# Linear attention's weight preparation moved to GpSimd and to earlier layers of a four-layer decoder

## The chip, the cores and the metric

The kernel runs on one core of one Trainium2 chip, as one launch. The metric is the device time of one execution in microseconds. Three runs of the kernel before took 2272.78, 2275.60 and 2278.18 us; the median is 2275.6.

## The reference

Four decoder layers run over x, 8 sequences of 128 tokens by 256 features in fp32. Each layer adds three sublayers to x, each of the layer-normalised x. The change touches three that follow each other:

- **L1_ffn** (the expert stage): a shared gated feed-forward and seven routed ones, top 3 by a softmax router; the gates weigh the experts' outputs.
- **L2_attn** (ALiBi attention): 16 heads of 16, causal, with a slope per head.
- **L2_xattn** (called linear attention below, after its quantised linear layers): `ln_out` is quantised four times, `y = clip(ln_out / in_scale, -448, 448)` rounded to bf16 and then to the grid of float8 e4m3, for q, qx, k and v. Then q, k, v, qx are linear in those, k and v of the context `kx, vx` are linear in `cond`; q, k, qx and kx are layer-normalised per head of 128; 16 heads attend to 8 k/v groups, once to the sequence and once to the context; both results are quantised again and multiplied by `wproj`.

```
q  = ln(fp8_linear(ln_out, wq, wq_scale, q_in_scale))      # 16 heads x 128
k  = ln(fp8_linear(ln_out, wk, wk_scale, k_in_scale))      #  8 heads x 128
xq = round_fp8(clip(x / in_scale)); fp8_linear = (xq * in_scale) @ w.T * w_scale
out = quantise(concat(core, xout), proj_smooth) @ wproj.T * (proj_in_scale * proj_w_scale)
```

The kernel folds `in_scale * w_scale` into the weights, and takes each head's mean out of the weights (centring) so that the layer norm of q, k, qx and kx needs only a sum of squares.

## The kernel before

One program per engine is written out by hand; engines meet at semaphores only. Each engine runs its list in order, so the order of the lines is the order of the work. SyncE (SP) issues all DMAs from one queue. Names: L1f is the expert stage, L2a ALiBi attention, L2x linear attention.

**Expert stage (L1f).** Four passes `b` over two sequences each. PE does gate/up and down products for eight experts; ACT the SiLU; DVE the products, the router's small tensors (7 columns: L2703 to L2748, among them L2734) and the weighted sums. GpSimd has no part in it. In its time GpSimd runs `L2x_split` (L1183 to L1194) for the eight pieces `q` of the output weight `wproj`: cast to bf16 (`hi`), subtract, cast (`mid`), subtract, cast (`lo`), so that three bf16 matmuls stand for one of fp32. The pieces come through two buffers `p_raw`; SP loads piece q when `lo` of q - 2 is done.

**ALiBi attention (L2a).** A software pipeline of nine iterations; the sequence is the index. On GpSimd iteration i is norm(i + 2) (L1204), then two subtractions of the row maximum (L1208), one for each half of the heads. ACT: copies of transposed tiles, two exp (L1743), the copy of the next normalised sequence (L1725). DVE: bias (L2831), maximum (L2837), reciprocal (L2841), scale, residual (L2849). PE: scores, transposes, products, projection (L4049). At its end PE, DVE and POOL wait for all of it.

**Linear attention (L2x).** First an opening: DVE takes sequence 0's statistics and normalises it (`L2x_stats`, `L2x_u`), PE transposes, ACT scales (`L2x_unT`), DVE and GpSimd quantise it four times in turn (`L2x_quantise`, four DVE instructions; `L2x_quantise_sum`, two on GpSimd, L1226 and L1228). ACT scales the weights of step j (`L2x_scale_weights`, L1788 and L1791, one head at a time with a sum), DVE subtracts the means (`L2x_centre_weights`, L2898 to L2904). Steps 0 and 1 are in the opening, steps 2 to 7 in iterations 0 to 5 of the loop.

Then 64 iterations (n = i // 8 is the sequence, i % 8 the group of heads, own keys for the first four and context keys for the others). In an iteration: project q, k, v (L4096, L4100, L4108), squares on ACT and their sum on DVE (L2925), rstd, norm, transposes, scores, exp (L1844), `L2x_prob` on GpSimd (L1232), product with v, `L2x_smooth` (DVE, L2947 to L2955, rounding the output), `L2x_cat` (GpSimd, L1238, L1240), and the projection of iteration i - 3 with the three bf16 weights (L4157). In iterations with i % 8 from 3 to 6 DVE and GpSimd quantise the next sequence.

SP (L964 to L992) loads the weights of L2x into the place of the expert stage's weights, so it waits for that stage's last matmuls and last vector work; the ten loads were issued between 747.5 and 756.5 us.

Of the kernel before, what the change touches and what calls it, by code (L numbers as in the profile page):

```python
# [108 lines left out]
def build_program(nc, dram, out_d):  # L109
# [89 lines left out]
    with stack:  # L199
# [259 lines left out]
        w_q2 = view(sbuf, 18376, [2, 2048])  # L459
        w_qx2 = view(sbuf, 22472, [2, 2048])  # L460
        w_k2 = view(sbuf, 14274, [2, 1024])
        w_v2 = view(sbuf, 16322, [2, 1024])
        w_kv2 = view(sbuf, 26568, [2, 2048])
        p_raw = [view(sbuf, 11520 + 1024 * p, [4, 256]) for p in range(2)]
        w_p3 = [view(sbuf, 30664 + 4096 * p, [32, 256], BF16) for p in range(3)]
# [6 lines left out]
        wsum = view(sbuf, 42984, [2, 12])  # L472
        wmean = view(sbuf, 43008, [2, 12])
# [8 lines left out]
        L2a_P = [view(sbuf, 46152 + 1024 * a, [8, 128]) for a in range(2)]  # L482
# [14 lines left out]
        L2a_u = view(sbuf, 44040, [256])  # L497
# [32 lines left out]
        wps = view(sbuf, 52838, [1])  # L530
# [13 lines left out]
        L2x_uT = view(psum, 3840, [2, 128])  # L544
        L2x_qT = view(psum, 1024, [4, 128])
# [286 lines left out]
        rest_done = stack.enter_context(nc.semaphore('rest_done'))  # L832
        L2x_w_loaded = stack.enter_context(nc.semaphore('L2x_w_loaded'))
# [23 lines left out]
        def _(sp):  # L857
# [99 lines left out]
            sp.dma_start(w_dn1[:, :, :, :], w_dn1_d).then_inc(L1f_w_loaded, 16)  # L957

# [22 lines left out]
            sp.wait_ge(L1f_w_loaded, 112)  # L981
            sp.dma_start(w_k2[:, :, :], w_k2_d).then_inc(L2x_w_loaded, 16)
            sp.wait_ge(L1f_matmul_done, 138)
            sp.dma_start(w_v2[:, :, :], w_v2_d).then_inc(L2x_w_loaded, 16)
            sp.wait_ge(L1f_w_loaded, 112)
            sp.wait_ge(L1f_vector_done, 221)
            sp.dma_start(w_kv2[:, :, :], w_kv2_d).then_inc(L2x_w_loaded, 16)
            sp.dma_start(insc[:, :, :], insc_d).then_inc(L2x_w_loaded, 16)
# [12 lines left out]
            sp.wait_ge(L0f_w_loaded, 64)  # L1001
            sp.dma_start(w_q2f[:, :], w_q2f_d).then_inc(L2f_w_loaded, 16)
# [52 lines left out]
        def _(pool):  # L1055
# [127 lines left out]
            def L2x_split(q):  # L1183
                part = slice(4 * q, 4 * q + 4)
                pool.wait_ge((L2x_p0_loaded, L2x_p1_loaded)[q % 2], 16 * (q // 2) + 16)
                pool.tensor_copy(w_p3[0][:, part, :], p_raw[q % 2][:, :, :]).then_inc(hi_done, 1)
                pool.wait_ge(hi_done, L2x_start['hi'] + q + 1)
                pool.tensor_tensor(p_raw[q % 2][:, :, :], p_raw[q % 2][:, :, :], w_p3[0][:, part, :], ALU.subtract).then_inc(rest_done, 1)
                pool.wait_ge(rest_done, 2 * q + 1)
                pool.tensor_copy(w_p3[1][:, part, :], p_raw[q % 2][:, :, :]).then_inc(mid_done, 1)  # L1190
                pool.wait_ge(mid_done, L2x_start['mid'] + q + 1)
                pool.tensor_tensor(p_raw[q % 2][:, :, :], p_raw[q % 2][:, :, :], w_p3[1][:, part, :], ALU.subtract).then_inc(rest_done, 1)
                pool.wait_ge(rest_done, 2 * q + 2)
                pool.tensor_copy(w_p3[2][:, part, :], p_raw[q % 2][:, :, :]).then_inc(lo_done, 1)  # L1194

            pool.wait_ge(resid_done, L1x_start['resid'] + 8)
            for q in range(8):
                L2x_split(q)
# [18 lines left out]

            pool.wait_ge(L0f_w_loaded, 64)
            pool.wait_ge(proj_done, L2a_start['proj'] + 8)
            pool.memset(keys[:, :, :], 0.0).then_inc(L2f_keys_zeroed, 1)  # L1220
# [23 lines left out]
            for i in range(67):  # L1244
# [4 lines left out]
                if i < 56 and i % 8 in (3, 4, 5, 6):  # L1249
                    L2x_quantise_sum(4 * (i // 8 + 1) + i % 8 - 3)  # L1250

# [84 lines left out]
        def _(act):  # L1336
# [379 lines left out]

            def L2a_rstd(a, b, c):
# [54 lines left out]
            act.wait_ge(L2x_w_loaded, 160)  # L1772

            def L2x_scale_weights(j):
                act.wait_ge(const_done, L2x_start['const'] + 1)
                if j >= 2:
                    act.wait_ge(centred_done, L2x_start['centred'] + j - 1)
                g, part = j % 4, j // 4
                wq, vq = (w_q2, 0) if part == 0 else (w_qx2, 1)
                wk = w_k2 if part == 0 else w_kv2  # L1780
                if part == 0:
                    for c in range(2):
                        w = w_v2[:, c, 256 * g:256 * g + 256]
                        act.activation(w, w, ACT.Copy, scale=wfs[:, 3, c:c + 1])
                for c in range(2):
                    for h in range(4):
                        w = wq[:, c, 512 * g + 128 * h:512 * g + 128 * h + 128]
# [70 lines left out]
            for i in range(66):  # L1858
# [12 lines left out]
                if i < 6:  # L1871
                    L2x_scale_weights(i + 2)
# [2911 lines left out]
```

## Time and profile before

| what | value |
|---|---|
| median of three runs | 2275.6 us |
| the profiled execution's own time | 2279.39 us |
| its span, first to last instruction | 2277.6 us |
| mean granted TensorE clock, share of full | 0.927 |
| busy: PE, DVE, ACT, POOL | 1897.8, 1494.5, 1111.4, 1027.5 us |
| expert stage's four passes | 575.5 to 754.3 us |
| ALiBi attention | 754.3 to 852.5 us |
| linear attention: opening, then 64 iterations | 852.5 to 872.4, then to about 1450 us |
| splitting of the output weight on GpSimd | 575.4 to 636.7 us |

Busy time is the time in which an engine carries out instructions. The granted clock is the share of its full speed that TensorE was given. The chain of work that ended last, over the whole span, is PE 45%, DVE 22%, issue 12%, ACT 11%, POOL 9%.

### The profile page before, as it was taken

Reading aid. Unit: us, or ns where it says so; the run is one execution under the profiler, and the core shown is the slowest. Engines: PE = TensorE matmul, PEld = TensorE weight load, DVE = VectorE, ACT = ScalarE, POOL = GpSimd, SP = SyncE. Lnnn points to the kernel's source line nnn. Section 1 sums busy time; section 2 is a strip of 40 time slices with the busy share of each in tenths; the row PEclk is TensorE's granted clock in tenths of the full one; section 3 lists DMA queues with packets and bytes.
Section 4 is the critical chain, followed back from the end, with each engine's and each line's share of the span. In section 5 each row is a group of like instructions: output and inputs, shape, how many; then the busy total and the mean of one; then the engine's idle time right before and its main releaser. Section 6 shows DMA issues by size and latency. Waiting matters only on the chain.

```text
span 2277.6 us, 32744 instructions
## 1 busy us (share of the span) xinstructions
PE 1897.8 (83%) x11446; PEld 1395.2 (61%) x11446; DVE 1494.5 (66%) x2588; ACT 1111.4 (49%) x2532; POOL 1027.5 (45%) x734
## 2 busy tenths in 40 slices
PE   7677788787999875699999999768888789977999
PEld 6111166544899663577777777657777665544888
DVE  5698933475654573566666666569999958756443
ACT  4444422253232346666565665556766536633443
POOL 2699921121910331344454444479999920012231
PEclk9688888698999996899999999989999989998999
DMA  4111001201100301000000000100000020000000
GB/s 153 42 33 33 0 1 72 111 0 56 56 0 0 149 5 55 1 1 1 1 1 1 1 1 22 34 1 1 1 1 1 26 76 1 1 0 1 6 8 8
DMA packets 22164, 54.82 MB, mean 24 GB/s; under 512 B 8463, under 2 KB 13752, under 8 KB 19592
## 3 DMA queue, kind: packets, MB, share of 16 engines
q1 hardware_dynamic: 22024, 53.01, 7.0%
q8 instruction: 81, 1.33, 0.2%
q14 instruction: 59, 0.48, 0.1%
HBM read 44.61 MB, written 1.05 MB: 20 GB/s over the span
## 4 chain that ended last, share of the span: by engine, by line
PE 45%; DVE 22%; issue 12%; ACT 11%; POOL 9%; SPq 1%; DMA 0%; DVEq 0%; POOLq 0%; ACTq 0%
POOL sbuf L1270 4%; DVE sbuf L2255 3%; PE psum L4096 3%; DVE sbuf L2925 3%; PE psum L4157 2%; POOL sbuf L1278 2%; PE psum L3475 2%; ACT sbuf L1844 2%; PE psum L4144 2%; DVE psum L3060 1%; PE psum L4583 1%; PE psum L4604 1%; PE psum L4590 1%; DVE sbuf L2917 1%; PE psum L4100 1%
## 5 line engine op out<-in xcount | busy, mean ns | idle before, releaser
L1270 POOL TENSOR_TENSOR sbuf<-sbuf 128x1035 f32<-128x1035 f32 x128 | 248.4, 1971 | 0.9 <-ACT sbuf L1912 0.9
L4230 PE MATMUL psum<-sbuf 128*128 128x128 f32 (+1 forms) x1024 | 143.3, 290 | 58.7 <-ACT sbuf L1921 43.0
L1921 ACT ACTIVATE sbuf<-sbuf 128x1001 f32<-128x1001 f32 (+1 forms) x128 | 141.6, 1139 | 100.8 <-DVE sbuf L3068 65.0
L4230 PEld LDWEIGHTS psum<-sbuf 128*128 128x128 f32 (+1 forms) x1024 | 125.6, 152 | 79.8 <-ACT sbuf L1921 58.1
L1232 POOL TENSOR_TENSOR sbuf<-sbuf 128x512 f32<-128x512 f32 x64 | 69.6, 1087 | 217.2 <-DVE sbuf L2942 217.2
L1111 POOL TENSOR_TENSOR sbuf<-sbuf 128x1024 f32<-128x1024 f32 x64 | 149.9, 2354 | 16.1 <-DVE sbuf L2255 15.2
L2255 DVE TENSOR_TENSOR_SCAN sbuf<-psum,sbuf 128x1024 f32<-128x1024 f32 x64 | 144.5, 2278 | 14.0 <-POOL sbuf L1111 7.7
L3423 PE MATMUL psum<-sbuf 96*128 96x512 bf16 x256 | 83.9, 439 | 74.3 <-DVE sbuf L2255 33.1
L4096 PE MATMUL psum<-sbuf 128*128 128x512 f32 x256 | 124.3, 609 | 17.4 <-DVE sbuf L2904 17.4
L3060 DVE SCALAR_TENSOR_TENSOR psum<-sbuf,psum 128x1024 f32<-128x1024 f32 (+1 forms) x96 | 122.3, 1274 | 14.2 <-PE psum L4220 7.0
L1391 ACT ACTIVATE psum<-psum,sbuf 128x1016 f32<-128x1016 f32 x64 | 68.9, 1081 | 125.5 <-PE psum L3423 125.5
L1844 ACT ACTIVATE sbuf<-psum,sbuf 128x128 f32<-128x128 f32 x256 | 90.7, 366 | 77.1 <-DVE sbuf L2936 77.1
L3068 DVE TENSOR_TENSOR sbuf<-psum,sbuf 128x1024 f32<-128x1024 f32 (+1 forms) x96 | 116.4, 1213 | 3.3
L4144 PE MATMUL psum<-sbuf 128*128 128x256 f32 x256 | 74.3, 414 | 52.0 <-ACT sbuf L1851 52.0
L3423 PEld LDWEIGHTS psum<-sbuf 96*128 96x128 bf16 x256 | 19.0, 104 | 152.5 <-DVE sbuf L2255 62.5
L1238 POOL TENSOR_TENSOR sbuf<-sbuf 128x512 f32<-128x512 bf16 x64 | 74.3, 1161 | 68.2 <-DVE sbuf L2955 66.5
L4157 PE MATMUL psum<-sbuf 128*128 128x256 bf16 x768 | 98.2, 280 | 5.0 <-POOL sbuf L1240 5.0
L4157 PEld LDWEIGHTS psum<-sbuf 128*128 128x128 bf16 x768 | 76.8, 100 | 24.1 <-POOL sbuf L1240 6.1
L1325 POOL TENSOR_TENSOR sbuf<-sbuf 128x1024 f32<-128x1024 f32 x16 | 30.3, 1915 | 129.6 <-DVE sbuf L3315 129.6
L2925 DVE TENSOR_REDUCE sbuf<-sbuf 128x6 f32<-128x768 f32 x64 | 60.8, 950 | 38.4 <-ACT sbuf L1814 38.4
L4144 PEld LDWEIGHTS psum<-sbuf 128*128 128x128 f32 x256 | 44.5, 194 | 67.5 <-ACT sbuf L1851 63.9
L1240 POOL TENSOR_TENSOR sbuf<-sbuf 128x512 bf16<-128x512 f32 x64 | 81.3, 1271 | 5.0
(899 smaller groups left out, 5153.6 us busy)
## 6 DMA issues: line engine op xcount, KB each, us to landing
sbuf<-sbuf SPq DMA_DIRECT2D x42, 128.0 KB, 2.4
sbuf<-w_p_d SPq DMA_DIRECT2D x8, 512.0 KB, 3.6
sbuf<-w_qkv_d SPq DMA_DIRECT2D x3, 768.0 KB, 4.3
sbuf<-w_e_d SPq DMA_DIRECT2D x1, 2048.0 KB, 7.7
sbuf<-w_gu_d SPq DMA_DIRECT2D x1, 2048.0 KB, 9.4
sbuf<-w_gu_d SPq DMA_DIRECT2D x2, 1024.0 KB, 7.9
sbuf<-w_dn_d SPq DMA_DIRECT2D x1, 2048.0 KB, 16.4
sbuf<-w_q_d SPq DMA_DIRECT2D x1, 2048.0 KB, 8.3
```

The lines of the kernel that those rows point to most:

```text
L1111: pool.tensor_tensor(L0a_hc[i % 4][:, :], L0a_hs[i % 2][:, :], L0a_Cr[g % 4][:, :], ALU.mult).then_inc(hc_done, 1)
L1270: pool.tensor_tensor(P_r[g % 7][:, :, :], rows.unsqueeze(2).to_broadcast([128, 23, 45]), cols.unsqueeze(1).to_broadcast([128, 23, 45]), AL ...
L1844: last = act.activation(prob[:, h, :], L2x_s[:, h, :], ACT.Exp, bias=smax[:, h:h + 1], accum_out=esum[:, h:h + 1])
L1921: act.activation(Q_r[g % 6][:, 0:w], Q_r[g % 6][:, 0:w], ACT.Silu, scale=q8_p[n % 2][:, h:h + 1]).then_inc(silu_done, 1)
L2255: dve.tensor_tensor_scan(L0a_hs[i % 2][:, :], L0a_dAf[i % 2][:, :], L0a_us[i % 3][:, :], 0.0, ALU.mult, ALU.add).then_inc(scan_done, 1)
L2925: dve.tensor_reduce(ssum[:, :], sq[:, :, :], AX.X, ALU.add).then_inc(ss_done, 1)
L3060: dve.scalar_tensor_tensor(M[:, 0:w], Pf_r[g % 7][:, o:o + w], t8_p[n % 2][:, h, 7:8], zps[:, 0:w], ALU.is_ge, ALU.mult).then_inc(mask_don ...
L3068: dve.tensor_tensor(Q_r[g % 6][:, 0:w], Mps[:, 0:w], Pf_r[g % 7][:, o:o + w], ALU.mult).then_inc(prod_done, 1)
L4096: last = pe.matmul(L2x_q[:, :, :], xs[:, vq, c, :], wq[:, c, 512 * g:512 * g + 512], start=c == 0, stop=c == 1)
L4144: last = pe.matmul(L2x_o[:, 2 * h:2 * h + 2, :], v2_r[i % 3][:, h, :], pT2[:, 2 * h:2 * h + 2, :], start=True, stop=True)
L4157: last = pe.matmul(L2x_out[:, :], cat16[:, h, :], w_p3[p][:, 4 * (i % 8) + h, :], start=i % 8 == 0 and h == 0 and p == 0, stop=i % 8 == 7 ...
L4230: last = pe.matmul(Gps[0:m, c, :], Q_r[g % 6][:, 128 * c:128 * c + m], ident[:, :], start=h == 0 and c % 4 == 0, stop=h == 7, skip_group_c ...
```

## The change

- **Scaling and centring** of w_v, w_k, w_q, w_qx and w_kv leave ACT and DVE; GpSimd does all of it after the ALiBi table, in the time of the expert stage. A scale is one product over 8 or 16 heads of 128; a mean is a tree of seven additions in place of ACT's running sum.
- **The split** of the output weight is shared: casts `hi` and `mid` on ACT, subtractions `rest` and `lo` on GpSimd (`lo` writes bf16 at once, its own cast is gone). Pieces 0 to 3 go into the iterations of ALiBi attention, 4 to 7 into iterations 0 to 7 of linear attention, one of `rest` and `lo` an iteration.
- **Sequence 0**: statistics in DVE's iteration 3 of ALiBi attention, u(0) and copies 0 and 1 in iteration 7, copies 2 and 3 in iteration 8; the transpose goes to another PSUM tile. PE's wait for the whole of ALiBi attention goes.
- **Buffers**: the L2x weights move behind the expert stage's, so they are loaded once L1_xattn's residuals are done; the split weight takes the place of the expert stage's weights. Two buffers of ALiBi attention move.
- **SP**: insc, wsc, w_k and w_v are issued with the expert stage's own weights; pieces 2 to 7 of the output weight come behind the L2x weights, and the loads of the next layer (L997 on) behind them. `keys` is zeroed in iteration 8 of linear attention.

```diff
-        w_q2 = view(sbuf, 18376, [2, 2048])
+        w_q2 = view(sbuf, 30664, [2, 2048])
-        w_p3 = [view(sbuf, 30664 + 4096 * p, [32, 256], BF16) for p in range(3)]
+        w_p3 = [view(sbuf, 18376 + 4096 * p, [32, 256], BF16) for p in range(3)]
 SP
+            sp.dma_start(w_k2[:, :, :], w_k2_d).then_inc(L2x_c_loaded, 16)
+            sp.dma_start(w_v2[:, :, :], w_v2_d).then_inc(L2x_c_loaded, 16)
...
-            sp.wait_ge(L1f_matmul_done, 130)
+            sp.wait_ge(resid_done, L1x_start['resid'] + 8)
             sp.dma_start(w_q2[:, :, :], w_q2_d).then_inc(L2x_w_loaded, 16)
...
+            for q in range(2, 8):
+                sp.wait_ge(lo_done, L2x_start['lo'] + q - 1)
+                sp.dma_start(p_raw[q % 2][:, :, :], w_p2_d[:, 4 * q:4 * q + 4, :]).then_inc((L2x_p0_loaded, L2x_p1_loaded)[q % 2], 16)
 GpSimd
+            def L2x_scale(j, w, factor):
+                pool.tensor_tensor(w, w, factor.unsqueeze(2).to_broadcast([128, w.shape[1], 128]), ALU.mult).then_inc(scaled_done, 1)
+            def L2x_centre(j, w, heads):
+                pool.tensor_tensor(wtree[:, 0:heads, 0:64], w[:, :, 0:64], w[:, :, 64:128], ALU.add).then_inc(sums_done, 1)
+                for s in range(6):
+                    half = 32 >> s
+                    pool.wait_ge(sums_done, L2x_start['sums'] + 8 * j + s + 1)
+                    pool.tensor_tensor(wtree[:, 0:heads, 0:half], wtree[:, 0:heads, 0:half], wtree[:, 0:heads, half:2 * half], ALU.add).then_inc(sums_done, 1)
...
+                pool.tensor_scalar(wmean[:, 0:heads], wtree[:, 0:heads, 0], -1.0 / 128.0, None, ALU.mult).then_inc(sums_done, 1)
...
+                pool.tensor_tensor(w, w, wmean[:, 0:heads].unsqueeze(2).to_broadcast([128, heads, 128]), ALU.add).then_inc(centred_done, 1)
...
+            def L2x_rest(q):
+                part = slice(4 * q, 4 * q + 4)
                 pool.wait_ge(hi_done, L2x_start['hi'] + q + 1)
                 pool.tensor_tensor(p_raw[q % 2][:, :, :], p_raw[q % 2][:, :, :], w_p3[0][:, part, :], ALU.subtract).then_inc(rest_done, 1)
+            def L2x_lo(q):
...
+                pool.tensor_tensor(w_p3[2][:, part, :], p_raw[q % 2][:, :, :], w_p3[1][:, part, :], ALU.subtract).then_inc(lo_done, 1)
 GpSimd, ALiBi attention, end of iteration i
                 L2a_sub(i, 0)
                 L2a_sub(i, 1)
+                if i % 2 == 0:
+                    L2x_rest(i // 2)
+                else:
+                    L2x_lo(i // 2)
 ACT, ALiBi attention, end of iteration i
+                if i % 2 == 0:
+                    if i == 0:
+                        act.wait_ge(L1f_matmul_done, 138)
+                    L2x_hi(i // 2)
+                else:
+                    L2x_mid(i // 2)
+                if i == 5:
+                    L2x_factor(0)
+                if i == 7:
+                    act.wait_ge(L2x_w_loaded, 96)
+                    L2x_unT(0)
 ACT, linear attention
-                if i < 6:
-                    L2x_scale_weights(i + 2)
+                if i % 2 == 1 and i < 8:
+                    L2x_mid(4 + i // 2)
+                    if i < 7:
+                        L2x_hi(5 + i // 2)
 GpSimd, linear attention, end of iteration i
+                if i < 8:
+                    if i % 2 == 0:
+                        L2x_rest(4 + i // 2)
+                    else:
+                        L2x_lo(4 + i // 2)
 DVE, ALiBi attention
+                if i == 7:
+                    L2x_u(0)
                 if i > 0:
                     L2a_scale(i - 1)
                     L2a_resid(i - 1)
+                if i == 7:
+                    L2x_quantise(0)
+                    L2x_quantise(1)
...
+                if i == 8:
+                    L2x_quantise(2)
+                    L2x_quantise(3)
 PE
-            pe.wait_ge(resid_done, L2a_start['resid'] + 8)
...
-                if n == 0:
-                    pe.wait_ge(centred_done, L2x_start['centred'] + i + 1)
+                if i == 0:
+                    pe.wait_ge(centred_done, L2x_start['centred'] + 8)
...
-                if i == 0:
-                    pe.wait_ge(lo_done, L2x_start['lo'] + 8)
+                if i < 8:
+                    pe.wait_ge(lo_done, L2x_start['lo'] + i + 1)
```

## Rows read from the trace of the kernel before

**Rows 1.** The page's busy time, share of span and instructions by engine.
```profile
PE 1897.8 (83%) x11446; PEld 1395.2 (61%) x11446; DVE 1494.5 (66%) x2588; ACT 1111.4 (49%) x2532; POOL 1027.5 (45%) x734
```

**Rows 2.** Windows by stage: us, busy by engine, granted clock, DMA share.
```profile
575.50:622.70 47.20, 44.40 (x334) 41.89 (x333) 30.35 (x62) 11.63 (x30) 45.38 (x32) 1.00 0.22 58
622.70:667.10 44.40, 43.20 (x327) 41.07 (x326) 24.29 (x62) 11.34 (x29) 13.48 (x9) 1.00 0.03 10
667.10:710.90 43.80, 43.80 (x335) 41.86 (x334) 19.73 (x63) 11.76 (x29) 0.00 (x0) 1.00 0.00 0
...
754.30:852.50 98.20, 78.83 (x976) 63.32 (x976) 66.86 (x86) 43.60 (x69) 40.41 (x25) 0.94 0.16 66
852.50:872.40 19.90, 0.66 (x2) 0.29 (x2) 9.26 (x31) 12.06 (x56) 6.57 (x9) 0.50 0.53 167
872.40:975.50 103.10, 73.73 (x311) 53.55 (x312) 52.30 (x113) 63.94 (x269) 24.43 (x25) 0.81 0.00 1
975.50:1044.70 69.20, 63.19 (x373) 49.37 (x372) 46.64 (x93) 41.65 (x133) 34.21 (x33) 1.00 0.00 1
```

**Rows 3.** Waits, 852 to 976 us: total us, times, longest.
```profile
DVE sbuf L2898 <- ACT sbuf L1791: 25.8, 6, 5.2
...
PE psum L4096 <- DVE sbuf L2904: 17.4, 1, 17.4
```

**Rows 4.** Groups of instructions, 852 to 976 us: busy us, mean ns.
```profile
L1788 ACT ACTIVATE sbuf<-sbuf 128x128 f32<-128x128 f32 x64 | 24.8, 397 | 0.0
```

**Rows 5.** Timeline of PE: start us, us, line; the first projection.
```profile
872.42 3.78 PE L4096 MATMUL psum<-sbuf 128*128 128x512 f32 x4 [17.45 <-DVE sbuf L2904]
```

**Rows 6.** Timeline of DVE and GpSimd in the opening.
```profile
852.05 0.42 DVE L2849 TENSOR_TENSOR sbuf<-psum,sbuf 128x256 f32<-128x256 f32 x1 [1.70 <-PE psum L4049]
...
867.56 0.72 POOL L1228 TENSOR_TENSOR sbuf<-sbuf 128x256 f32<-128x256 f32 x1
```

**Rows 7.** Timeline of ACT and GpSimd in ALiBi attention.
```profile
775.52 1.05 ACT L1743 ACTIVATE sbuf<-sbuf 128x1024 f32<-128x1024 f32 x1
...
784.27 1.05 ACT L1743 ACTIVATE sbuf<-sbuf 128x1024 f32<-128x1024 f32 x1
...
788.78 1.90 POOL L1208 TENSOR_TENSOR sbuf<-sbuf 128x1024 f32<-128x1024 f32 x1 [3.84 <-DVE sbuf L2837]
...
793.51 1.22 POOL L1204 TENSOR_SCALAR sbuf<-sbuf 128x256 f32<-128x256 f32 x1
...
793.88 1.05 ACT L1743 ACTIVATE sbuf<-sbuf 128x1024 f32<-128x1024 f32 x1
...
794.82 0.38 ACT L1725 ACTIVATE sbuf<-psum 128x256 f32<-128x256 f32 x1
```

**Rows 8.** Timeline of GpSimd and DVE in the expert stage.
```profile
575.43 1.03 POOL L1186 CAST sbuf<-sbuf 128x1024 bf16<-128x1024 f32 x1
...
576.55 2.13 POOL L1188 TENSOR_TENSOR sbuf<-sbuf 128x1024 f32<-128x1024 f32 x1
...
584.17 2.14 POOL L1188 TENSOR_TENSOR sbuf<-sbuf 128x1024 f32<-128x1024 f32 x1
584.28 2.06 DVE L2734 TENSOR_TENSOR sbuf<-sbuf 128x7 f32<-128x7 f32 x1
...
676.40 0.17 DVE L2734 TENSOR_TENSOR sbuf<-sbuf 128x7 f32<-128x7 f32 x1
```

**Rows 9.** Timeline of GpSimd and DVE in linear attention.
```profile
1069.28 1.04 POOL L1232 TENSOR_TENSOR sbuf<-sbuf 128x512 f32<-128x512 f32 x1 [3.38 <-DVE sbuf L2942]
...
1080.41 0.81 POOL L1228 TENSOR_TENSOR sbuf<-sbuf 128x256 f32<-128x256 f32 x1
...
1080.67 0.70 DVE L2953 TENSOR_SCALAR sbuf<-sbuf 128x512 uint16<-128x512 uint16 x1
...
1081.75 0.94 DVE L2925 TENSOR_REDUCE sbuf<-sbuf 128x6 f32<-128x768 f32 x1
```

**Rows 10.** DMA issues, 440 to 760 us: KB each, us to landing.
```profile
sbuf<-w_kv_d SPq DMA_DIRECT2D x1, 2048.0 KB, 16.2
```

More of the change, by code:

```diff
@@ L481, in build_program @@
         L2a_table = view(sbuf, 9472, [2, 8, 128])
-        L2a_P = [view(sbuf, 46152 + 1024 * a, [8, 128]) for a in range(2)]
+        L2a_P = [view(sbuf, 3328 + 1024 * a, [8, 128]) for a in range(2)]
         L2a_PT = [view(sbuf, 48200 + 1024 * a, [8, 128]) for a in range(2)]
@@ new lines, in _ @@
+            for c in range(2):
+                pool.wait_ge(scaled_done, L2x_start['scaled'] + 3 + c)
+                L2x_centre(c, L2x_heads(w_k2[:, c, :]), 8)
+            pool.wait_ge(L2x_w_loaded, 96)
+            for c in range(2):
+                L2x_scale(4 + c, L2x_heads(w_q2[:, c, :]), wfs[:, 0, c:c + 1])
+            for c in range(2):
+                pool.wait_ge(scaled_done, L2x_start['scaled'] + 5 + c)
+                L2x_centre(2 + c, L2x_heads(w_q2[:, c, :]), 16)
+            for c in range(2):
+                L2x_scale(6 + c, L2x_heads(w_qx2[:, c, :]), wfs[:, 1, c:c + 1])
@@ L1184, in L2x_split @@
+            for c in range(2):
+                pool.wait_ge(scaled_done, L2x_start['scaled'] + 7 + c)
+                L2x_centre(4 + c, L2x_heads(w_qx2[:, c, :]), 16)
+            for c in range(2):
+                L2x_centre(6 + c, L2x_heads(w_kv2[:, c, 0:1024]), 8)
+            def L2x_rest(q):
                 part = slice(4 * q, 4 * q + 4)
-                pool.wait_ge((L2x_p0_loaded, L2x_p1_loaded)[q % 2], 16 * (q // 2) + 16)
-                pool.tensor_copy(w_p3[0][:, part, :], p_raw[q % 2][:, :, :]).then_inc(hi_done, 1)
@@ L1193, in L2x_split @@
[L1193 to L1198, printed above, removed]
+                pool.tensor_tensor(w_p3[2][:, part, :], p_raw[q % 2][:, :, :], w_p3[1][:, part, :], ALU.subtract).then_inc(lo_done, 1)
             def L2a_norm(n):
@@ L1771, in _ @@
                     L2a_unTc(i + 2)
[L1772 to L1787, printed above, removed]
-                        act.activation(w, w, ACT.Copy, scale=wfs[:, vq, c:c + 1], accum_out=wsum[:, j % 2, 4 * c + h:4 * c + h + 1])
-                    for h in range(2):
-                        w = wk[:, c, 256 * g + 128 * h:256 * g + 128 * h + 128]
-                        last = act.activation(w, w, ACT.Copy, scale=wfs[:, 2, c:c + 1] if part == 0 else 1.0, accum_out=wsum[:, j % 2, 8 + 2 * c + h:9 + 2 * c + h])
-                last.then_inc(scaled_done, 1)
@@ L3989, in _, with L2x_uTr @@
                 last.then_inc(L1f_matmul_done, 1)
+            def L2x_uTr(n):
+                pe.wait_ge(u_done, L2x_start['u'] + n + 1)
+                out = L2x_uT_first if n == 0 else L2x_uT
+                for c in range(2):
+                    last = pe.transpose(out[:, c, :], u0[:, 128 * c:128 * c + 128], ident[:, :])
+                last.then_inc(uT_done, 1)
             def L2a_uTr(n):
@@ L4073, in _ @@
                     L2a_project(i - 1)
-            pe.wait_ge(resid_done, L2a_start['resid'] + 8)
-            def L2x_uTr(n):
-                pe.wait_ge(u_done, L2x_start['u'] + n + 1)
-                for c in range(2):
-                    last = pe.transpose(L2x_uT[:, c, :], u0[:, 128 * c:128 * c + 128], ident[:, :])
-                last.then_inc(uT_done, 1)
+                if i == 7:
+                    L2x_uTr(0)
             def L2x_project(i):
```

180 lines of the change are left out of this document (82 added, 98 removed).

## The prediction

> **What bounds the kernel now.** I read the stages first. The page gives PE as the busiest engine, 83% of a span of 2277.6 us [rows 1], but an average over twelve layers prices nothing. The table of windows [rows 2] cuts out the stretch that the change touches: the four passes of the expert stage (575.5 to 754.3 us), ALiBi attention (754.3 to 852.5), the opening of linear attention (852.5 to 872.4) and its 64 iterations. Two rows stand out. In the opening PE is busy 0.66 of 19.9 us. The first eight iterations take 103.1 us where the next eight take 69.2, though both do the same attention work and both quantise the sequence that follows; PE's granted clock is 0.81 in the first and full in the second. So 19.9 + 33.9 = 53.8 us are spent on what the change moves: scaling and centring the weights, and quantising sequence 0.
>
> The waits of that stretch say who makes the time [rows 3]. PE waits 17.4 us for the first centred group (L2904), and DVE's centring (L2898) waits 25.8 us for ACT's scaling, which is 96 short instructions with an accumulator read behind each; 64 of them (L1788) alone are 24.8 us plus their reads [rows 4]. ACT is the bound there; after the weights are done its load is gone.
>
> **The change, part by part.** All sums are against the profiled execution (span 2277.6 us, 2279.4 us with what lies around it); the median of the runs is 2275.6, 3.8 us lower, and a difference worked out on the trace is taken off the median.
>
> *1. Weights out of the first eight iterations: -32.7 us.* From the first projection, at 872.42 [rows 5], to the ninth, at 975.5, are 103.1 us [rows 2]. Eight iterations without weights take 69.2 [rows 2]; I add 1.2 for the first, which starts on a slow clock (3.78 us for its first four matmuls, [rows 5]), and get 70.4. The difference is 32.7. Bounds of the 70.4: 68 (a pipeline that fills is shorter) and 76 (the clock stays at 1.2 GHz for two iterations).
>
> *2. Sequence 0 quantised inside ALiBi attention: -13.6 us.* Before, the last residual ends at 852.47 and the third quantised copy, the one that the first projection waits for, then as now, at 868.28 [rows 6]; centring brings the start to 872.42. After, u(0), the transpose and copies 0 and 1 stand in iterations 7 and 8. They aren't free: the fourth `lo` on GpSimd has two SBUF inputs, and the first copy's DVE multiply has too, so by the kind of wait in [rows 8] it starts when `lo` ends, near 847.4. That copy is 1.3 us, its GpSimd sum 1.5, and copy 1's second half (0.9) waits for it, so DVE reaches the last normalisation at 851.3 where it stood at 848.1, +3.2 us. Residual 7 ends at 855.7, copy 2 takes 1.4 and its sum 1.5 more, and the projection starts at 858.8 instead of 872.4. Bounds 11 and 17 (the latter if DVE comes through copy 1 before attention's last product is ready).
>
> *3. Split of the output weight inside ALiBi attention: +6.2 us.* Nothing here is a bound engine: GpSimd is busy 40 and ACT 44 of 98 us [rows 2]. But GpSimd runs in order. In iteration i it now does norm(i+2), two subtractions, then `rest` or `lo`, which wait for a cast on ACT that stands behind exp(i,1) and the copy L1725. Queued behind that wait is norm(i+3), then the subtraction that iteration i+1 needs. From [rows 7]: exp(i,1) at 793.88, L1725 ends at 795.20, cast 1.05 (an ACT pass over 1024 elements, as exp), GpSimd from 796.3, 2.14 for `rest` (as L1188, [rows 8]), norm 1.22, so the subtraction starts at 799.6, where today it comes 9.8 us behind the one at 788.78, at 798.6. From the subtraction to the next exp(i,1) are 5.1 us, as from 788.78 to 793.88: the loop through ACT and GpSimd is 10.8 us with `rest` and some 11.0 with `lo`, against 9.8 us. It binds where a norm is in it, in the steps to iterations 1 to 5: 2.1 for the first (8.75 before, 784.27 less 775.52), 1.1 for each of four, 6.5, of which PE's idle time ahead of the projection L4049 gives back some 0.5 (an estimate); u(0) adds 0.35 in iteration 7, the reciprocals and the statistics fall into idle time of DVE (0.68 us an iteration). Bounds 0.5 (GpSimd's norm slips through; no gain, since nothing is taken out of these iterations) and 9.
>
> *4. Scaling and centring on GpSimd in the expert stage: +4 us.* Work: 1 + 8 + 8 x 9 = 81 instructions over 36,768 elements a partition. By L1208 (1024 elements, 1.90 us, [rows 7]) and L1232 (512, 1.04, [rows 9]) an element costs 1.68 ns and an instruction 0.18, and 0.09 lies between two that depend on each other (576.46 to 576.55, [rows 8]): 84 us, from 575.5 to 660. It replaces 61 us of splitting and ends 94 us before ALiBi attention needs anything, so GpSimd's own time is free. What isn't free is DVE. In pass 0, under the split, one DVE product of 7 elements (L2734) takes 2.06 us, exactly until GpSimd's instruction ends; in pass 2, with GpSimd idle, it takes 0.17 [rows 8]. Over a pass that is 30.35 us of DVE against 19.73, and the pass is 47.2 us against 43.8; pass 1, covered for 14 us, is 44.4 [rows 2]. So the split costs 3.4 + 0.6 us now and 10.6 us of blocking turns into 3.4 of time. After, the k weights' short sums lie beside pass 0's routing (cheaper, about -2), but two shared products at its end and pass 1's whole routing meet instructions of 2048 elements, 3.6 us each. I take -1 for pass 0 and +5 for pass 1. Bounds -2 and +9.
>
> The row shows an exclusive wait, and the Trainium skill (SBUF — State Buffer, Who interferes with whom) says the same: GpSimd and a DVE instruction with two SBUF inputs, or in a two-port mode, hold the pair for a whole instruction. By that rule a wait grows with the length of GpSimd's instruction, which speaks against this change; were it of one size whatever the instruction, this term would be near 0 and the sum -29. The trace agrees with the rule: 2.06 us beside an instruction of 2.14.
>
> *5. The second half of the split inside linear attention: +11 us.* In iterations 0 to 7 GpSimd runs `rest` or `lo` (2.1 to 2.4 us) right behind the quantising sum. DVE then has the smoothing's three conversions (L2951, L2953, L2955), all SBUF to SBUF. Now L2953 takes 0.70 us because it waits for L1228, and the sum of squares L2925 follows at 1081.75 without a pause [rows 9]. With `rest` behind L1228, L2955 waits till 1083.4 and L2925 starts 2.1 us later, and it is on the path (chain: L2925, L1851, then PE). That is 4 x 2.2 for iterations 3 to 6, 0.8 each for 2 and 7, where DVE has a pause, and 0.7 for ACT's two casts in iteration 1: 11. Bounds: 3 (DVE's three conversions pass first; 0.4 each in eight iterations) and 17 (both delays in every iteration).
>
> *6. Transfers: 0.* The weights' 6 MB leave at 571 instead of 747.5; the last landed 16.2 us after issue [rows 10], before GpSimd gets to w_q at 594. If it were late, GpSimd has 94 us to spare. Queue SP is now held by `lo` until iteration 5 of linear attention before the next layer's weights; they have 500 us.
>
> Sum: -32.7 - 13.6 + 6.2 + 4 + 11 = -25.1, from the median 2275.6: **2250.5 us**.
>
> **Rivals.**
> *A. The cover holds* (terms 3 and 5 mostly hidden): GpSimd is idle 58 us of ALiBi attention [rows 2], and if casts and subtractions slip into the gaps, terms 3 to 5 are 1, 1 and 4, and the time is 2235. Against it: GpSimd's order, and the gaps are after the norm, not ahead of it.
> *B. Contention costs more*: 9 + 8 + 17 with -12 and -30 of gain, the clock low for a while: 2268. For it: PE's clock was 0.81 when its work was broken up [rows 2].
> *C. Slower.* In the expert stage each of some ten shared DVE instructions a pass waits for a GpSimd instruction of 3.6 us, and none of it is hidden, over two passes: 20 x 2.6 = 52 us of wait less 4 paid today, +48 in place of +4, and the time is 2294. It decides from +29 on. Against it: only a third of pass 0's blocking reached the pass, and 2048-element instructions are under half of GpSimd's time.
> *D. It doesn't do what it says*: something else holds the first projection (GpSimd still centring, a late transfer), and only the ACT load goes: within 4.5 us of 2275.6. GpSimd's 94 us of reserve speak against it.
>
> **How the numbers follow.** Forecast 0.52 (2242 to 2259), A 0.20, B 0.22, C 0.03, D 0.03. The range 2234 to 2264 holds A's centre and the near half of B. 0.2% is 4.5 us, about what a measurement of this kernel tells from no change: faster 0.94, same 0.03, slower 0.03.
>
> **What would show it.** Right: the first L4096 projection near 869 us of the span and the ninth near 950; no ACT scaling in linear attention; ALiBi attention's iterations at 10.8 to 11.0 us for the first five and 9.8 after; pass 1 of the experts at 48 to 50 us with long DVE waits at its tiny products; iterations 3 to 6 of linear attention near 11.2 us. Wrong: iterations there of 9.05 (term 5 is nothing), ALiBi iterations of 9.8 (term 3 is nothing), or a projection that starts before 860 or after 880.

## The result and the profile after

The changed kernel takes 2331.7 us (median of 4 runs, 2327.85 to 2338.36), the kernel before 2275.8 (median of 4, 2272.78 to 2278.18): a ratio of 1.0251, 95% interval 1.0226 to 1.0275. It is 56 us slower where 25 us faster was predicted, far outside the range of 2234 to 2264. The profiled execution took 2338.36 us, its span is 2336.6; before, 2279.4 and 2277.6.

The busy line of the page answers to [rows 1] and shows nothing of it. PE has the same work, ACT and DVE have less, and GpSimd is busy 57 us more.

```profile
PE 1897.1 (81%) x11446; PEld 1397.0 (60%) x11446; DVE 1481.4 (63%) x2547; ACT 1088.7 (47%) x2348; POOL 1084.5 (46%) x791
```

The windows by stage of the kernel after, with the columns of [rows 2], show it at once. The first four are the passes of the expert stage, the fifth has no counterpart in [rows 2], then come ALiBi attention with the opening, and the first and second eight iterations of linear attention:

```profile
576.40:619.20 42.80, 42.80 (x326) 40.86 (x325) 19.53 (x62) 11.21 (x29) 0.17 (x1) 1.00 0.38 149
619.20:663.00 43.80, 43.80 (x335) 41.87 (x334) 19.73 (x63) 11.75 (x29) 0.00 (x0) 1.00 0.00 0
663.00:706.70 43.70, 43.70 (x334) 41.77 (x334) 19.66 (x63) 11.75 (x29) 0.00 (x0) 1.00 0.00 0
706.70:751.90 45.20, 42.20 (x319) 39.92 (x317) 21.40 (x73) 13.53 (x32) 0.02 (x1) 1.00 0.00 0
751.90:838.30 86.40, 0.00 (x0) 0.00 (x0) 2.23 (x12) 0.00 (x0) 81.27 (x81) 0.51 0.00 0
838.30:945.50 107.20, 78.53 (x978) 63.49 (x978) 69.17 (x86) 51.70 (x80) 61.22 (x38) 0.93 0.07 21
945.50:1027.10 81.60, 64.04 (x310) 46.76 (x311) 51.18 (x83) 43.83 (x128) 42.78 (x35) 0.90 0.10 33
1027.10:1096.30 69.20, 63.19 (x372) 49.36 (x371) 47.38 (x91) 41.65 (x133) 35.56 (x33) 1.00 0.09 26
```

For 86.40 us PE executes nothing and GpSimd is the only engine with work worth naming. In the expert stage, where that work was to be, GpSimd has one product of 0.20 us and then 175 us of nothing. Its timeline says why; the bracket is the idle time ahead of an instruction and what ended it:

```profile
566.71 9.69 POOL L1176 TENSOR_SCALAR sbuf<-sbuf 128x128 f32<-128x128 f32 x16
576.37 0.20 POOL L1197 TENSOR_TENSOR sbuf<-sbuf 128x8 f32<-128x8 f32 x1
751.88 7.45 POOL L1180 TENSOR_TENSOR sbuf<-sbuf 128x1024 f32<-128x1024 f32 x4 [175.32 <-DVE sbuf L2920]
...
836.39 1.90 POOL L1191 TENSOR_TENSOR sbuf<-sbuf 128x1024 f32<-128x1024 f32 x1
838.27 1.24 POOL L1235 TENSOR_SCALAR sbuf<-sbuf 128x256 f32<-128x256 f32 x1
```

L1197 is the product wfs (input scale times weight scale, one factor for each weight), L1180 the first scaling, L1191 the last centring, L1235 the first normalising of ALiBi attention. Between wfs and the first scaling stands L1198, `pool.wait_ge(const_done, L2x_start['const'] + 1)`: GpSimd waits for its own product. But `const_done` counts constants of all layers. `L2x_start['const']` is 9, so the wait wants ten. wfs made the ninth; the tenth comes from L2920, the last of VectorE's clears for ALiBi attention, which VectorE reaches when the last expert pass is over. Before, wfs was VectorE's and stood behind that clear, so the tenth increment was always its own. The early increment also works the other way, which no time here shows: VectorE (L2922) and PE (L4062) wait for the ninth count, which was the clear's, and wfs now gives it 175 us before the clear runs. The waits of 575 to 840 us put the rest in one line each (total, times, longest):

```profile
POOL sbuf L1180 <- DVE sbuf L2920: 175.3, 1, 175.3
PEld psum L4026 <- POOL sbuf L1235: 91.1, 1, 91.1
PE psum L4026 <- POOL sbuf L1235: 90.7, 1, 90.7
```

The work itself, 751.88 to 838.27, is 86.4 us; the prediction had 84. Nothing stands beside it, because the next thing that every engine needs is the normalising queued behind it.

**Where the time went**, stage by stage (us, from starts in the traces: first pass, first normalising, first and ninth projection of linear attention, first transposition and last residual of the feed-forward layer behind it). The last five columns are experiments, told below.

| stretch | before | after | own count | no weights | norm first | both | best |
|---|---|---|---|---|---|---|---|
| expert passes, to the first normalising | 181.3 | 262.7 | 181.2 | 176.3 | 181.3 | 181.2 | 176.5 |
| to the first projection | 116.4 | 107.3 | 108.5 | 110.7 | 102.8 | 102.8 | 104.0 |
| first eight iterations | 103.1 | 81.6 | 77.4 | 77.1 | 80.0 | 71.3 | 71.3 |
| to the next layer | 499.4 | 499.4 | 500.6 | 500.9 | 501.0 | 501.8 | 501.0 |
| feed-forward layer | 378.7 | 386.2 | 383.9 | 383.1 | 383.2 | 381.0 | 383.5 |
| from there to the end | 424.0 | 423.9 | 424.0 | 424.2 | 424.0 | 423.9 | 425.7 |

After against before: +0.9 ahead of the passes, +81.4, -9.2, -21.5, 0, +7.5, -0.1, together the +59.0 of the two spans. The gains that were forecast are there (-30.7); 81.4 us of exposed GpSimd work lie over them.

### The profile page after: what moved, and what is told of

Its sections match the earlier page's. It is cut to its first block, busy times and chain, and to the rows that moved or that the text cites. A ratio compares the mean times of both kernels' runs of the same rounds, so it can differ in the third digit from the quotient of the medians.

```text
span 2336.6 us, 32570 instructions
## 1 busy us (share of the span) xinstructions
PE 1897.1 (81%) x11446; PEld 1397.0 (60%) x11446; DVE 1481.4 (63%) x2547; ACT 1088.7 (47%) x2348; POOL 1084.5 (46%) x791
## 4 chain that ended last, share of the span: by engine, by line
PE 43%; DVE 21%; POOL 13%; issue 12%; ACT 9%; SPq 1%; DMA 0%; DVEq 0%; POOLq 0%; ACTq 0%
POOL sbuf L1308 4%; DVE sbuf L2288 3%; DVE sbuf L2962 3%; PE psum L4119 3%; DVE psum L3082 2%; PE psum L4180 2%; PE psum L3497 2%; ACT sbuf L1879 2%; PE psum L4167 2%; PE psum L4605 1%; DVE sbuf L3090 1%; DVE sbuf L2870 1%; POOL sbuf L1316 1%; PE psum L4626 1%; PE psum L4612 1%
## 5 line engine op out<-in xcount | busy, mean ns | idle before, releaser
L4252 PEld LDWEIGHTS psum<-sbuf 128*128 128x128 f32 (+1 forms) x1024 | 130.5, 157 | 78.4 <-ACT sbuf L1954 59.4
L3090 DVE TENSOR_TENSOR sbuf<-psum,sbuf 128x1024 f32<-128x1024 f32 (+1 forms) x96 | 116.4, 1213 | 3.3
L1180 POOL TENSOR_TENSOR sbuf<-sbuf 128x1024 f32<-128x1024 f32 (+1 forms) x8 | 21.8, 2747 | 175.3 <-DVE sbuf L2920 175.3
L3476 PE MATMUL psum<-sbuf 128*32 128x512 f32 x256 | 81.4, 769 | 3.5 <-POOL sbuf L1107 3.5
```

What stands on the lines that cost most here:

```text
L3090: dve.tensor_tensor(Q_r[g % 6][:, 0:w], Mps[:, 0:w], Pf_r[g % 7][:, o:o + w], ALU.mult).then_inc(prod_done, 1)
L4252: last = pe.matmul(Gps[0:m, c, :], Q_r[g % 6][:, 128 * c:128 * c + m], ident[:, :], start=h == 0 and c % 4 == 0, stop=h == 7, skip_group_c ...
```

## The experiments

The theory (W): the wait on the shared count is the whole of the loss; with a count of its own the work runs beside the experts, and the forecast's sum holds. The rivals: GpSimd's work disturbs the other engines wherever it stands (C, the one of the prediction), or the early count does harm in itself.

**e1_own_count** gives wfs a count of its own: it counts on top of the four loads that it waits for, and the shared counter gets its tenth increment from a constant that VectorE computes in ALiBi attention:

```diff
-            pool.tensor_tensor(wfs[:, :, :], ..., ALU.mult).then_inc(const_done, 1)
-            pool.wait_ge(const_done, L2x_start['const'] + 1)
+            pool.tensor_tensor(wfs[:, :, :], ..., ALU.mult).then_inc(L2x_c_loaded, 1)
+            pool.wait_ge(L2x_c_loaded, 65)
...
-                    dve.tensor_tensor(wps[:, :], wsc[:, 4:5], wsc[:, 5:6], ALU.mult)
+                    dve.tensor_tensor(wps[:, :], wsc[:, 4:5], wsc[:, 5:6], ALU.mult).then_inc(const_done, 1)
```

> Only the count that GpSimd waits on is changed: its product of the scales counts on the semaphore of its own loads (65th count) instead of the const_done shared with ALiBi attention, whose count for this stage is given by VectorE's product wps in ALiBi attention. Theory W (the loss is GpSimd's wait on the shared count, 576 to 752, with the whole of the weights' work after it): GpSimd works on the weights from 576 to about 660-665 beside the expert passes, the first normalising starts near 756-760 instead of 838, the first projection near 867, and the time falls by about 78-82 us from 2332, to 2250-2254. Theory C (GpSimd's work on the weights disturbs VectorE and ScalarE wherever it stands): the expert passes stretch by 20 us or more, the time is 2275-2295.

Measured: 2249.2 us (before 2274.4 beside it; ratio 0.9882, 0.9865 to 0.9900). The same GpSimd lines as above, now 92.94 us of rest behind the work instead of 175 ahead of it:

```profile
573.62 0.20 POOL L1197 TENSOR_TENSOR sbuf<-sbuf 128x8 f32<-128x8 f32 x1
573.89 7.45 POOL L1180 TENSOR_TENSOR sbuf<-sbuf 128x1024 f32<-128x1024 f32 x4
...
659.26 1.90 POOL L1191 TENSOR_TENSOR sbuf<-sbuf 128x1024 f32<-128x1024 f32 x1
754.10 1.24 POOL L1235 TENSOR_SCALAR sbuf<-sbuf 128x256 f32<-128x256 f32 x1 [92.94 <-ACT sbuf L1781]
```

Three changed lines took 82.5 us off (2331.7 to 2249.2; the ratios to before, 1.0251 and 0.9882, leave no room for chance). W is shown; rival C falls: the passes and what follows them take 181.2 us, as before.

**e2_no_weights** is e1 without the 81 instructions of scaling and centring; **e7_wait_no_work** is the changed kernel, its wait kept, also without them. The first prices the work where it is hidden, the second asks whether the wait costs anything when nothing stands behind it.

> As e1_own_count, but GpSimd's scaling and centring of the weights is left out altogether, so linear attention computes with unscaled weights. The difference from e1_own_count is what the weights' work costs beside the expert passes. Theory W with my term of 4 us: e1_own_count is 3-5 us slower than this (this at 2246-2250). Theory C: the difference is 20-40 us. If the work costs nothing there: the two are the same.

> The changed kernel with its wait on the shared count left as it is, but without the scaling and centring behind it, so linear attention computes with unscaled weights. Theory W2 (the wait by itself costs nothing; what costs is that 86 us of weights' work stand behind it, ahead of the first normalising): GpSimd waits until about 745-752 and the time is that of e2_no_weights, 2241-2247. Rival (the wait or the early count disturbs in itself, for instance by the memory port or the order of attention): 2255 or more.

Measured: 2243.7 us (ratio 0.9862, 0.9844 to 0.9880) and 2248.1 (0.9861, 0.9841 to 0.9881), the same against before. In the second GpSimd rests 175.36 us and the first normalising starts at 751.88, where the scaling started in the kernel after. So the rival of the early count falls too: the wait is free and the work is nearly free; what cost 82 us is the one behind the other. The windows of the expert stage up to the first normalising, of e1, e2 and the kernel before, in this order:

```profile
572.90:754.10 181.20, 174.35 (x1314) 165.22 (x1312) 98.64 (x260) 48.72 (x119) 83.05 (x83) 1.00 0.09 35
```
```profile
568.50:744.80 176.30, 173.32 (x1314) 165.21 (x1312) 80.58 (x260) 48.73 (x119) 0.91 (x3) 1.00 0.09 36
```
```profile
574.70:756.00 181.30, 174.37 (x1314) 165.51 (x1312) 96.01 (x260) 48.80 (x119) 59.69 (x43) 1.00 0.10 33
```

The same 260 VectorE instructions take 80.58 us alone and 98.64 beside GpSimd; of these 18 us, 4.9 reach the stage. The kernel before, with its split in that place, has 5.0 us more than e2 in the same way.

**e3_norm_first** moves the normalising of ALiBi attention ahead of the split; **e4_both** moves also the split in linear attention ahead of the probabilities, and spreads ScalarE's casts:

```diff
             L2a_norm(0)
             L2a_norm(1)
+            L2a_norm(2)
             for i in range(8):
-                if i < 6:
-                    L2a_norm(i + 2)
                 L2a_sub(i, 0)
                 L2a_sub(i, 1)
+                if i < 5:
+                    L2a_norm(i + 3)
```
```diff
                 if i >= 3:
                     L2x_cat(i - 3)
+                if i < 8:
+                    if i % 2 == 0:
+                        L2x_rest(4 + i // 2)
+                    else:
+                        L2x_lo(4 + i // 2)
                 if 1 <= i < 65:
                     L2x_prob(i - 1)
                 ...
-                if i < 8:
-                    ... L2x_rest / L2x_lo as above
@@ ScalarE
-                if i % 2 == 1 and i < 8:
-                    L2x_mid(4 + i // 2)
-                    if i < 7:
-                        L2x_hi(5 + i // 2)
+                if i < 8:
+                    if i % 2 == 0:
+                        L2x_mid(4 + i // 2)
+                    elif i < 7:
+                        L2x_hi(5 + i // 2)
```

> e1_own_count, and in ALiBi attention GpSimd normalises sequence i+3 ahead of the output weight's rest or lo of iteration i, instead of behind it. Theory N (the split's cost there is GpSimd standing between the subtractions and the next normalising, some 1.1 us an iteration in the first five): 5-6 us faster than e1_own_count, the ALiBi iterations at 9.8 us again. Rival: ScalarE's casts (1.05 us an iteration) are what lengthens them, then no difference.

> e3_norm_first, and in linear attention's first eight iterations GpSimd does rest and lo right behind the concatenation instead of last, and ScalarE casts once in an iteration instead of twice in every second. Theory S (iterations 3 to 6 take 10.8 us instead of 8.2-9.1 since the split stands at the end of GpSimd's order and delays the next concatenation): 7-10 us faster than e3_norm_first, near 2236. Rival Q (what lengthens these is the quantisation of the next sequence, which before overlapped the scaled weights and is in the same iterations): under 2 us.

Measured: 2245.5 us (0.9863, 0.9841 to 0.9884) and 2234.0 (0.9821, 0.9802 to 0.9839). GpSimd's order in two ALiBi iterations, in e1 and then in e3 (L1223 and L1228 are `rest` and `lo`, L1235 the normalising, L1239 the subtraction):

```profile
786.74 2.14 POOL L1228 TENSOR_TENSOR sbuf<-sbuf 128x1024 bf16<-128x1024 f32 x1 [3.68 <-ACT sbuf L1775]
788.88 1.21 POOL L1235 TENSOR_SCALAR sbuf<-sbuf 128x256 f32<-128x256 f32 x1
790.06 3.74 POOL L1239 TENSOR_TENSOR sbuf<-sbuf 128x1024 f32<-128x1024 f32 x2
797.49 2.13 POOL L1223 TENSOR_TENSOR sbuf<-sbuf 128x1024 f32<-128x1024 f32 x1 [3.68 <-ACT sbuf L1771]
```
```profile
783.78 1.22 POOL L1235 TENSOR_SCALAR sbuf<-sbuf 128x256 f32<-128x256 f32 x1 [0.75 <-PE psum L4027]
786.69 2.15 POOL L1228 TENSOR_TENSOR sbuf<-sbuf 128x1024 bf16<-128x1024 f32 x1 [1.69 <-ACT sbuf L1776]
788.79 1.90 POOL L1239 TENSOR_TENSOR sbuf<-sbuf 128x1024 f32<-128x1024 f32 x1
...
793.32 1.22 POOL L1235 TENSOR_SCALAR sbuf<-sbuf 128x256 f32<-128x256 f32 x1 [0.40 <-PE psum L4027]
```

From `lo` to the next `rest` are 10.75 us (786.74 to 797.49) with the normalising behind them. With it ahead, the iterations, read at VectorE's residuals (one in each; L2912, 784.50 to 794.29), are 9.79 us apart, as in the kernel before (L2849, 785.11 to 794.90). So the rival of e3, ScalarE's casts, falls: they are still there. The first projection comes 5.7 us earlier behind the first normalising (108.5 to 102.8). The first eight iterations give 2.6 of it back, so that e3 is 3.1 us ahead of e1 at the ninth. In time 5 to 6 us were expected; the medians are 3.7 apart, and the two can't be told apart (their intervals overlap). e4 brings these iterations from 80.0 to 71.3 us, so its rival, the quantisation, which is still there, falls as well. Its two edits, GpSimd's order and ScalarE's casts, were not run apart. How it works can be read on VectorE's last conversion of the smoothing. First the kernel after, then e4, GpSimd and VectorE of the same place:

```profile
996.43 2.17 POOL L1223 TENSOR_TENSOR sbuf<-sbuf 128x1024 f32<-128x1024 f32 x1
...
996.65 2.24 DVE L2992 TENSOR_SCALAR sbuf<-sbuf 128x512 f32<-128x512 bf16 x1
998.81 0.94 DVE L2962 TENSOR_REDUCE sbuf<-sbuf 128x6 f32<-128x768 f32 x1
```
```profile
892.89 0.43 DVE L2994 TENSOR_SCALAR sbuf<-sbuf 128x512 f32<-128x512 bf16 x1
893.23 0.94 DVE L2964 TENSOR_REDUCE sbuf<-sbuf 128x6 f32<-128x768 f32 x1
...
895.86 2.13 POOL L1223 TENSOR_TENSOR sbuf<-sbuf 128x1024 f32<-128x1024 f32 x1
```

After, the conversion takes 2.24 us because `rest` holds it, and the reduction for the next iteration waits behind it; iterations 3 to 6 take 9.9 to 10.9 us. In e4 it takes 0.43, since `rest` starts 2.5 us after it, and those iterations take 9.0 to 9.4.

**e5_halves, e6_kv_first, e8_best** go for the 4.9 us in the expert stage: GpSimd's instructions of 2048 elements cut in two, w_kv centred ahead of w_qx, and both. **e4_again** is e4 unchanged, on the chip of e5 and e6.

```diff
-                pool.tensor_tensor(w, w, wmean[:, 0:heads].unsqueeze(2).to_broadcast([128, heads, 128]), ALU.add).then_inc(centred_done, 1)
+                for a in range(0, heads, 8):
+                    last = pool.tensor_tensor(w[:, a:a + 8, :], w[:, a:a + 8, :], wmean[:, a:a + 8].unsqueeze(2).to_broadcast([128, 8, 128]), ALU.add)
+                last.then_inc(centred_done, 1)
```

> e4_both once more, unchanged, as the measure for the next two on the same chip: 2229-2238. A wider spread would say that differences of 3 us can't be told.

> e4_both with GpSimd's instructions of 2048 elements (and their first fold of 1024) cut into two of 1024 (and 512), the same elements in all and some 12 instructions more. Theory L (a VectorE instruction with two SBUF operands or in a fast form waits until the GpSimd instruction ends, so the wait is as long as that instruction): pass 1 of the experts falls from 47.6 to 45.5-46.5 us, VectorE's waits of 3.6-3.8 us at its short instructions become 1.9 at most, the time falls by 1-2 us. Rival F (the wait is a share of GpSimd's busy time, whatever the size): no change in pass 1 or +0.3.

> e4_both with the centring of w_kv (instructions of 1024 elements at most) ahead of the scaling and centring of w_qx (2048), so that pass 1's routing meets the short ones. By theory L pass 1 takes 45.5-46.5 us instead of 47.6 and the time falls by 1-2 us; if only the total of GpSimd's work beside a pass counts, pass 1 stays at 47.6.

> e4_both with both edits of the expert stage: instructions of 1024 elements, and w_kv centred ahead of w_qx. Theory L: the four passes and what lies up to the first normalising take 180.1 or less (181.23 in e4_both, 180.50 with the halves, 180.06 with w_kv first, 176.3 without the work); the time is 2229-2237. It adds up if 179.3 is read.

Measured, with the length of the stage up to the first normalising: e4_again 2240.4 us, 181.2; e5 2234.0, 180.5; e6 2239.9, 180.1; e8 2237.2, 176.5. A pass by itself can't be read to 2 us here, since records at its edge are missing in some traces; the whole can. The two edits do little one by one (-0.7, -1.2) and all of it together (-4.8): in sum the stage is as short as without the work. That is no sum of two shares, as e8's expectation had it. VectorE is still held there, though by less: its busy time in e4's stage, then in e8's.

```profile
570.10:751.30 181.20, 174.32 (x1314) 165.25 (x1312) 98.63 (x260) 48.80 (x119) 83.09 (x84) 1.00 0.09 35
```
```profile
573.80:750.20 176.40, 173.51 (x1314) 165.15 (x1312) 93.12 (x260) 48.79 (x119) 84.87 (x95) 1.00 0.09 36
```

With 93.12 us VectorE still loses 12.5 us to GpSimd (80.58 in e2), and none of it reaches PE. What counts is which instructions are held: in e4 a normalising for the next pass (L2792), which stands ahead of the product that PE waits for next (L2794), took 3.77 us, to the end of a GpSimd instruction of 3.61; the same kind of instruction just ahead of it took 0.40.

```profile
631.94 0.40 DVE L2791 TENSOR_SCALAR sbuf<-sbuf 128x256 f32 x1
632.27 3.77 DVE L2792 TENSOR_SCALAR sbuf<-sbuf 128x256 f32 x1
...
632.28 3.61 POOL L1191 TENSOR_TENSOR sbuf<-sbuf 128x2048 f32<-128x2048 f32 x1
...
635.96 0.41 DVE L2794 TENSOR_TENSOR sbuf<-sbuf,psum 128x256 f32<-128x256 f32 x1
```

Cut in two, the longest such wait is 1.94 us (the costliest VectorE group of e5 in pass 1; busy, mean ns):

```profile
L2753 DVE TENSOR_SCALAR sbuf<-sbuf 128x7 f32<-128x7 f32 x1 | 1.9, 1939 | 0.0
```

So theory L holds for the size of a wait; what it does for the stage depends on the order too. In time, e8 (ratio 0.9818, 0.9793 to 0.9843) is not to be told from e4 (0.9821) or e5 (0.9811, 0.9795 to 0.9826): its 4.7 us in the experts are given back in pieces, the largest 2.5 in the feed-forward layer, where two profiles of e4 differ by more (381.0 and 384.5). Times don't settle differences of a few us: e4_again has a ratio of 0.9844 (0.9831 to 0.9858), above its expected time of 2229 to 2238 us, with the code of e4. e5, run beside it, is 6.3 us faster, where 1 to 2 were expected and its stage shows 0.7; the rest isn't explained. Each of e4, e5 and e8 is some 40 us faster than the kernel before and 94 to 98 faster than the changed one.

**b_again, b_late3, b_late5** look at that layer, which no edit touches and which is 2 to 8 us longer in every kernel with the change.

> The kernel before, unchanged, for a second profile. In its first profile the feed-forward stage behind linear attention takes 280.8 us from its first to its last transposition; in the nine profiles of kernels with the change it is 284.1 to 288.1, with the same code. If that is something of the change (a buffer, a transfer), this profile gives 280-281 again; if it is where the granted clock falls in a run, it gives something up to 286.

> The kernel before, with five clears of VectorE buffers that are not yet in use added between ALiBi and linear attention (3072 elements a partition, some 3 us). Nothing else changes, so the layers behind start some 3 us later. Two profiles of the kernel before give 378.7 and 378.8 us from the first transposition to the last residual of the feed-forward stage behind linear attention; ten with the change give 381.0 to 386.2 with the same code, at a granted clock that is 0.01 to 0.02 lower there. Theory P (the clock's low stretches fall on other work when the start is moved): 381 to 386 here too. Rival T (something of the change, a buffer's place or a transfer): 378.7 again.

> As b_late3 with four clears of PSUM buffers more (1792 elements, some 5 us in all). Theory P: the feed-forward stage takes 381 to 386 us, and not the same as in b_late3 where the low stretches fall elsewhere. Rival T: 378.7 again.

Measured: 378.8, 378.3 and 379.2 us for the layer (times 2277.9, 2276.6 and 2285.0, one run each). The clears lengthen the way from the first normalising to the first projection by 3.8 and 5.1 us against the first profile (3.0 and 4.3 against b_again); since b_late3's first pass begins 7.8 us earlier than in the first profile, the layer starts at 1471.7 and 1480.0 us, against 1474.9. Moving its start by itself doesn't lengthen it, so theory P falls, as far as so small shifts go; in the kernels with the change the shift is 34 to 52 us. The two values are those of rival T (something of the change itself, a buffer's place or a transfer), which no run tests. Two things can be seen to differ. One is the granted clock: the fourth of the layer's sequences, and the whole layer, in the kernel before and in e3.

```profile
1584.90:1626.30 41.40, 35.64 (x254) 30.56 (x253) 39.52 (x60) 28.28 (x41) 40.58 (x22) 1.00 0.00 1
1474.90:1853.60 378.70, 302.39 (x2000) 260.87 (x2000) 326.18 (x477) 233.77 (x318) 326.31 (x168) 0.94 0.02 6
```
```profile
1549.80:1594.80 45.00, 38.24 (x252) 33.78 (x251) 42.59 (x61) 30.22 (x42) 42.23 (x22) 0.92 0.00 0
1439.00:1822.20 383.20, 306.28 (x2000) 264.74 (x2000) 329.66 (x477) 234.17 (x318) 326.27 (x168) 0.93 0.02 6
```

The sequence takes 41.4 us at full clock and 45.0 at 0.92. But b_late3 has 0.93 over the layer as well and takes 378.3. The other is VectorE's normalising of that fourth sequence, first in the kernel before, then in e3, where it lasts until GpSimd's two instructions beside it end (1546.58):

```profile
1579.45 0.59 DVE L3013 TENSOR_SCALAR sbuf<-sbuf 128x256 f32<-128x256 f32 x1
```
```profile
1542.73 3.85 POOL L1309 TENSOR_TENSOR sbuf<-sbuf 128x1035 f32<-128x1035 f32 x2
1544.52 2.20 DVE L3036 TENSOR_SCALAR sbuf<-sbuf 128x256 f32<-128x256 f32 x1
```

It takes 0.58 to 0.60 us in the four profiles without the change, b_late3's too, and 2.17 to 2.21 in all ten with it; from it to the next one are 42.6 us in the four and 44.2 to 44.8 in the ten. That is 1.6 to 2.1 of the 2 to 8 us, in the same place each time. Such a wait can therefore be part of the cost. Whether the held instruction makes the sequence longer, and why it meets GpSimd otherwise with the change, stays open.

## Why the prediction was wrong

**The step that failed** is in part 4: "It replaces 61 us of splitting and ends 94 us before ALiBi attention needs anything, so GpSimd's own time is free." The 84 us were right (86.4); that they begin at 575.5 was taken from the place of the lines in GpSimd's order, without following the wait between wfs and the first scaling to all that increments its counter. The wait stands in the changed kernel one line under the product (L1198). The prediction gave one sentence to what moves past which queue and none to what this added wait waits for. GpSimd's reserve was then used twice more, against rival D and for the late transfers. Rival D named the right place (GpSimd still centring when the projection wants the weights) but priced it at nothing lost: it saw only the projection behind that work, not the normalising of ALiBi attention, which is queued behind it on the same engine. The 0.03 on slower went by a mechanism, contention, that costs nothing net. The price of the missed case could be had from the prediction's own terms: 2275.6, GpSimd's 84 us behind the last pass, and -29.1 for terms 1, 2, 3 and 5 make 2330.5 us; 2331.7 was measured. Part of that match is luck: by the stages the exposed work is +81.4 and not +84, the other terms -30.7, and +8.3 us come from places that no term had.

**The other steps**, read in e1, where the wait is gone, and in e3 and e4:

- Term 1, weights out of the first eight iterations, -32.7: e4, with the split out of the way, has 71.3 us there against 103.1, -31.8. Right; the 70.4 were 0.9 low.
- Term 2, sequence 0 early, -13.6: e3 has the split out of ALiBi attention's path, and its first projection comes 102.8 us behind the first normalising against 116.4 before (872.42 in [rows 5], the normalising at 755.97), -13.6. Its +3.2 for VectorE is there too: the last residual comes 99.3 us behind the first normalising, and 96.1 before. Right.
- Term 3, split in ALiBi attention, +6.2 up to that projection: e1 less e3 is 5.7 us there, the iterations 10.75 us (one of them 12.38) where 10.8 to 11.0 were forecast. Right, though 2.6 us of it come back in the iterations behind.
- Term 4, expert stage, +4: 0.0 (181.2 against 181.3 us). The disturbance is 4.9 us as such; that the split had cost 5.0 in the same place was under-priced at 4.0.
- Term 5, split in linear attention, +11: e1 less e4 is 6.1 us, e3 less e4 8.7. The mechanism is the one forecast (L2992 held till `rest` ends, 2.24 us, the reduction behind it); iterations 3 to 6 were forecast at 11.2 and took 9.9 to 10.9.
- Part 6, transfers: nothing waited for one.
- Not forecast: 1.2 us more in the later iterations and 5.2 in the feed-forward layer, whose cause is open.

From these, e1 against before is 0.0 - 8.0 - 25.6 + 1.2 + 5.2 = -27.2, and -29.1 with the 1.8 us by which its first pass starts earlier. In medians it is -25.2, and the sum was -25.1. So near a match is partly luck: it owes something to terms 4 and 5, too dear by 4 and by 5, against the 6 us given back later.

The Trainium skill's rule that was weighed in part 4 (SBUF — State Buffer, Who interferes with whom) is borne out where the runs can tell: 3.77 us beside a GpSimd instruction of 3.61, and 1.94 at most once they are cut to 1.90.

## What to carry to other kernels

When a change moves or adds a wait, read the threshold as a number and list every increment that makes it up, on all engines and in program order: on a shared, cumulative counter an increment that is moved ahead of another one takes its number, and the wait that was its own turns into a wait for somebody else, while a wait written for the other is met too early. Then ask what is queued behind the waiting instruction, and price the case in which all of it starts when the last of those increments comes; that is the rival on the other side. When GpSimd is to work beside VectorE, keep its instructions short and its long ones away from VectorE's instructions that the bound engine waits for: in the expert stage here both together took off 4.8 us, one by one 0.7 and 1.2.

## What the runs showed of the hardware

- GpSimd's blocking of VectorE is not a tax by share of busy time. VectorE lost 18.1 us of busy time in e4's expert stage and the stage 4.9; it lost 12.5 in e8 and the stage nothing.
- PE stood still for 86.4 us, with a mean granted clock of 0.51 in that window (0.50, the lower level of 1.2 GHz, from 760 to 830 us). Over the next 107 us the mean was 0.93, where e1, without the pause, had 0.91; ALiBi attention paid nothing that could be measured for it (107.3 us, against 108.5 in e1).
- A layer whose code is the same took 378.3 to 379.2 us in four profiles of the kernel before and its two late variants, and 381.0 to 386.2 with the change in front of it, at a granted clock of 0.93 to 0.94 and 0.92 to 0.93. In the ten profiles of the second kind one VectorE instruction of it took 2.2 us, and 0.6 in the four of the first.
